# Four of the nine down products of the experts in three f32r passes, and the layer norm of their half on ScalarE

## The chip, the cores and the metric

One core of a Trainium2 chip runs the whole kernel. Its engines are TensorE (PE, with its weight loads as PEld), VectorE (DVE), ScalarE (ACT), GpSimd (POOL) and SyncE (SP, which here issues all the transfers). The metric is the device time of one execution in microseconds, and lower is better.

## What is computed

Two halves over 32 x 256 tokens of width 128, fp32 in and out, each a residual around a layer norm.

```python
x = x + attn(layernorm(x))          # 16 heads of 8, window of 128 keys
x = x + ffn(layernorm(x))           # below, per token

scores = sigmoid(x @ gate_w.T)                       # 16 experts
topk_idx, topk_weight = gate(scores)                 # best 2 of 4 groups, then best 4 experts
g = einsum('th,eih->eti', x, gate_proj)              # 64 inner units per expert
u = einsum('th,eih->eti', x, up_proj)
expert_out = einsum('eti,ehi->eth', silu(g) * u, down_proj)
y = sum over the 4 chosen of topk_weight * expert_out
shared = (silu(x @ shared_gate_w.T) * (x @ shared_up_w.T)) @ shared_down_w.T
return y + shared
```

All 16 experts are computed for every token. The weight of an expert that wasn't chosen is zero.

## The kernel before

The attention half runs first, in 16 steps of 512 tokens (`STEPS`, `TOK`), then the experts' half in 16 steps `d` of 512 tokens. What sets the order is the program text alone: each engine has its own queue, written out by hand, and counted semaphores between the queues.

A step of the experts' half has nine products `p`: eight pairs of experts (`NP` = 8, 2 x 64 inner units on 128 partitions) and the shared expert. For each of them:

- TensorE, `up(d, p)` (L1551): the gate and the up projection, each as three f32r passes. The operands were split beforehand into a high part, rounded to f32r, and a low part, the rest: `whigh`, `wlow` and `xh`, `xl`. The passes are high x high (L1560), high x low (L1561) and low x high (L1562), into `ps_max` and `ps_sc`, two banks each.
- ScalarE, `silus` (L769): silu of the gate projection.
- VectorE, `gate` (L1099): times the up projection, into one of two `gated` tiles.
- GpSimd, `weigh` (L612): times the routing weight, which has been spread over the partitions by a transfer (`spread`), into one of three tiles `inter`. It waits until the down product three before has freed the tile.
- TensorE, `down(d, p)` (L1565): one fp32 matmul with `wd`, added up in `ps_c` over the nine products. TensorE's queue holds it behind the up products of the third pair after: iteration `p` of the loop at L1644 issues `up(d, p)` and then the down product three before. In the iterations 0, 1 and 2 these are the last three down products of the step before.

Beside this, each step prepares others. Its layer norm for step d+3 has statistics on VectorE (L838, L845), then on GpSimd the inverse deviation (`inverse_deviation`, L497, in two 128x4 instructions), `centre` (L504) and `normalise` (L509) after the weighing of pairs 1, 2 and 3. TensorE transposes the result at p = 7 (`transpose_x1`), ScalarE copies its high part (`high_x`) and VectorE subtracts the low part (`low_x`). The routing for step d+2 has products on TensorE (`route`, at p = 1), two activations on ScalarE (`scores_of_experts`, after the silu of p = 3) and some thirty small instructions on VectorE between its gates: `sum_logits`, `clip` and `invert` after gate(2), `choices` (with `score` and `choice`) and `sum_pairs` after gate(3), the result of the step before (`add_y`) and `sum_groups` after gate(4), the group masks after gate(5), `find_best` and `mark_best` (with the copy `needles`) after gate(6), `choose_experts` (with `chosen`) and `shares` (with `total1`) after gate(7), then `gate_shared`. `up(d, p)` can't start before the gate two before it is done, since that frees its banks.

Between the halves, `last` interleaves the end of the attention with the transposes of the experts' weights (`transpose_weight`, L1475). ScalarE takes each bank (`take_weight`, L736) in the order router, shared, gate and up, down (two banks), and then the routing weights of step 0. These go to DRAM and come back spread over the partitions in a transfer of 1 MB (`store_weight`, `load_spread`), and the first `weigh` waits for it.


Of the kernel before, what the change touches and what calls it, by code (L numbers as in the profile page):

```python
# [6 lines left out]
FP32 = mybir.dt.float32  # L7
# [12 lines left out]
def build_block(nc, x, w_in, b_in, w_out, b_out, gate_w, e_bias, gate_proj, up_proj, down_proj,  # L20
# [46 lines left out]
    with ctx:  # L67
        def sb(name, shape, dt):
            return ctx.enter_context(nc.sbuf_tensor(name, shape, dt))
# [4 lines left out]
        def sem(name):  # L74
            return ctx.enter_context(nc.semaphore(name))
# [47 lines left out]


        NP = NE // 2
        TOPK, SCALING = 4, 2.5


# [12 lines left out]
        wlow = sb("wlow", [P, 2 * NP + 1, P], F32R)  # L141
        wrt = sb("wrt", [P, 2, NE], F32R)
        wd = sb("wd", [P, NP, E], FP32)
        wds = sb("wds", [I, E], FP32)
        xh = [sb(f"xh{p}", [P, TOK], F32R) for p in range(3)]
        xl = [sb(f"xl{p}", [P, TOK], F32R) for p in range(3)]
# [128 lines left out]
        gated_ready = sem("gated_ready")  # L275
        down_done = sem("down_done")
        inter_ready = sem("inter_ready")
        yT_ready = sem("yT_ready")
        y_tr_done = sem("y_tr_done")
        result_ready = sem("result_ready")  # L280
# [38 lines left out]
        def after(engine, semaphore, value):  # L319

            if value > 0:
                engine.wait_ge(semaphore, value)
# [153 lines left out]
        def _(pool):  # L476
            n_const = [0]

            def made():

                n_const[0] += 1
                return n_const[0]
# [10 lines left out]
            pool.wait_ge(const_ready, made())  # L493
            nc.gpsimd.memset(eps[:, :], EPS).then_inc(const_ready, 1)
            pool.wait_ge(const_ready, made())
            pool.sem_inc(ident_ready, 1)
            def inverse_deviation(i):  # L497

                pool.wait_ge(stats_ready, i + 1)
                nc.gpsimd.tensor_tensor(veps[:, :], meanvar[:, :, 1], eps[:, :], ALU.add).then_inc(pool_chain, 1)  # L500
                pool.wait_ge(pool_chain, 3 * i + 1)
                nc.gpsimd.tensor_tensor(rstd[:, :], veps[:, :], minus_half[:, :], ALU.pow).then_inc(pool_chain, 1)
# [96 lines left out]
            layer_norm(STEPS + 1)  # L599
            layer_norm(STEPS + 2)  # L600

            def scale_weight(d):

                if not valid(d):
                    return
                pool.wait_ge(share_ready, d + 1)
                after(pool, weight_tr_done, d)
                nc.gpsimd.tensor_tensor(weight[:, :, :], chosen[:, :, :],
                                        share[:, :].unsqueeze(2).to_broadcast([P, NT, NE]), ALU.mult
                                        ).then_inc(weight_ready, 1)  # L610
# [8 lines left out]
                                        ).then_inc(inter_ready, 1)  # L619

            scale_weight(0)
            scale_weight(1)
            for d in range(STEPS):
                more = d + 3 < STEPS
                for p in range(NP):
                    weigh(d, p)
                    if p == 1 and more:
                        inverse_deviation(STEPS + d + 3)
                    if p == 2 and more:
                        centre(STEPS + d + 3)  # L630
                    if p == 3 and more:
                        normalise(STEPS + d + 3)
                scale_weight(d + 2)


# [1 line left out]
        def _(act):  # L637
# [98 lines left out]
            def take_weight(n):  # L736
                dst, cols = WEIGHT_BANKS[n]
                act.wait_ge(fw_done, n + 1)
                rows = slice(0, {"sh_down": I, "weight": NE}.get(dst[0], P))
                nc.scalar.copy(high_of(dst), ps_max[n % 2][rows, 0:cols]).then_inc(fw_high, 1)  # L740


            def high_x(d):
# [25 lines left out]
            def silus(d, p):  # L769

                n = (NP + 1) * d + p
                act.wait_ge(g_done, n + 1)
                after(act, gated_ready, n - 1)
                rows = slice(0, P) if p < NP else slice(0, I)
                nc.scalar.activation(silu[n % 2][rows, :], ps_max[n % 2][rows, :], ACT.Silu).then_inc(silu_ready, 1)  # L775

            def take_y(d):

# [43 lines left out]
            for d in range(STEPS):  # L822
                if d > 0:
                    high_x(d + 2)
                for p in range(NP + 1):
                    silus(d, p)
                    if p == 2:
                        if d > 0:
                            take_y(d - 1)
                        take_weights(d + 1)  # L830
                    if p == 3:
                        scores_of_experts(d + 2)
# [390 lines left out]
        def _(pe):  # L1223
# [341 lines left out]
            def down(d, p):  # L1565

                if p == 0:
                    after(pe, yT_ready, d)
                if p < NP:
                    pe.wait_ge(inter_ready, NP * d + p + 1)  # L1570
                    last = mm(ps_c[:, :], wd[:, p, :], inter[p % 3], start=(p == 0), stop=False)  # L1571
                else:
                    pe.wait_ge(gated_ready, (NP + 1) * (d + 1))
                    last = mm(ps_c[:, :], wds[:, :], inter[p % 3][0:I, :], start=False, stop=True)  # L1574
                last.then_inc(down_done, 1)
# [64 lines left out]
            pe.wait_ge(probs_ready, 2 * UNITS * STEPS)  # L1640
            pe.wait_ge(fw_high, len(WEIGHT_BANKS))
            pe.wait_ge(fw_low, N_SPLIT)

            for d in range(STEPS):  # L1644
                for p in range(NP + 1):
# [40 lines left out]
```

## Time and profile before

| | us |
|---|---|
| median of 3 runs (756.61 to 762.22) | 761.21 |
| the profiled execution | 758.62 |
| its span, first to last instruction | 756.8 |
| experts' half, from its first down product to the end | 407.1 to 756.8 |
| mean granted clock of TensorE | 0.972 |

The rows come from the one profiled execution, so sums of rows are to be held against 758.62. "Busy" is the time in which an engine has an instruction running. A timeline row gives start, duration, engine, line, what is written from what is read, and the count of instructions merged in the row. Matmuls overlap in the records: a pass that holds the array for about 0.23 us is recorded as 0.39, so the pitch of the starts counts.

### The profile page before, as it was taken

To read this page: it belongs to the slowest core of one execution; us is meant where nothing else is said; L and a number is where in the kernel's file an instruction comes from. 1 tells how busy PE (TensorE), PEld (TensorE's weight loads), DVE (VectorE), ACT (ScalarE), POOL (GpSimd) and SP (SyncE) were. 2 spreads that over 40 slices of the span, in tenths; PEclk is the share of its full clock that TensorE was granted. 3 is DMA by queue.
4 is the path that set the end of the run, shared out by engine and by line. 5 is a ranking of instruction groups with operands and counts; after the bars stand their busy time and mean duration, and the time that the engine had idled before them with its cause. 6 is when DMAs were issued, how large, how long until landed. Compare 5 with 4: busy or idle time off the path is not lost.

```text
span 756.8 us, 21746 instructions
## 1 busy us (share of the span) xinstructions
PE 706.9 (93%) x8499; PEld 472.2 (62%) x8499; DVE 585.8 (77%) x1741; ACT 362.4 (48%) x739; POOL 306.4 (40%) x327
## 2 busy tenths in 40 slices
PE   4597999999999999999778999999999999999997
PEld 2365666666666666666555666666666666666664
DVE  6776788888888888888577878887777888777632
ACT  2165566767776676667562332333333233333321
POOL 6410221222211222122215656566666656664543
PEclk9589899999999999999999999999999999999999
DMA  2125123333323222333118366654445666544550
GB/s 59 58 87 148 62 85 102 102 102 102 101 61 101 86 70 93 102 102 101 59 35 207 73 138 154 155 134 113 118 122 137 152 155 120 131 103 108 119 139 29
DMA packets 64837, 79.96 MB, mean 106 GB/s; under 512 B 10960, under 2 KB 38880, under 8 KB 64736
## 3 DMA queue, kind: packets, MB, share of 16 engines
q1 hardware_dynamic: 64736, 78.58, 39.9%
q8 instruction: 68, 1.11, 0.6%
q14 instruction: 33, 0.27, 0.1%
HBM read 61.00 MB, written 17.56 MB: 104 GB/s over the span
## 4 chain that ended last, share of the span: by engine, by line
PE 80%; DVE 7%; DMA 5%; ACT 4%; issue 2%; SPq 1%; POOL 1%; DVEq 0%; ACTq 0%; PEldq 0%
PE ps_c L1571 14%; PE ps_att L1356 7%; PE ps_sc L1330 6%; PE ps_max L1288 5%; PE ps_max L1560 4%; PE ps_max L1562 4%; PE ps_max L1561 4%; PE ps_sc L1306 4%; PE ps_sc L1561 4%; PE ps_sc L1562 4%; PE ps_sc L1560 4%; PE ps_a L1254 3%; ACT probs L683 3%; PE ps_c L1574 2%; PE ps_b L1247 2%
## 5 line engine op out<-in xcount | busy, mean ns | idle before, releaser
L618 POOL TENSOR_TENSOR probs<-probs,stacks 128x512 f32<-128x512 f32 x128 | 165.0, 1290 | 125.7 <-DVE probs L1105 75.4
L775 ACT ACTIVATE probs<-ps_max 128x512 f32<-128x512 f32 x144 | 86.2, 598 | 220.1 <-PE ps_max L1562 216.5
L886 DVE TENSOR_REDUCE chunkmax<-ps_max 128x16 f32<-128x512 f32 (+1 forms) x256 | 155.3, 648 | 37.9 <-PE ps_max L1269 37.8
L683 ACT ACTIVATE probs<-ps_sc 128x512 f32<-128x512 f32 x256 | 138.9, 595 | 48.6 <-PE ps_sc L1306 47.6
L1105 DVE TENSOR_TENSOR probs<-probs,ps_sc 128x512 f32<-128x512 f32 x128 | 87.3, 682 | 69.6 <-PE ps_sc L1562 26.4
L1571 PE MATMUL ps_c<-probs,wd 128*128 128x512 f32 x256 | 130.3, 592 | 1.3 <-POOL probs L618 1.3
L1560 PE MATMUL ps_max<-xh,whigh 128*128 128x512 f32 x144 | 93.7, 650 | 2.9 <-DVE probs L1105 2.1
L531 POOL TENSOR_TENSOR xres<-xin,cvec 128x512 f32<-128x512 f32 x16 | 20.6, 1287 | 141.1 <-DVE x L938 140.7
L1330 PE MATMUL ps_sc<-stacks 32*64 32x192 f16 (+2 forms) x2048 | 64.4, 232 | 9.5 <-ACT probs L683 2.7
L1356 PE MATMUL ps_att<-probs,stacks 128*32 128x192 f32 (+1 forms) x1536 | 70.2, 317 | 0.0
L1288 PE MATMUL ps_max<-hl,qdiag 32*128 32x160 f16 (+4 forms) x1024 | 50.9, 220 | 16.0 <-DVE chunkmax L886 9.7
L1330 PEld LDWEIGHTS ps_sc<-stacks 32*64 32x64 f16 x2048 | 36.6, 105 | 42.2 <-ACT probs L683 27.0
L500 POOL TENSOR_TENSOR veps<-meanvar,eps 128x4 f32<-128x4 f32 x32 | 6.4, 201 | 136.7 <-DVE meanvar L850 136.7
L1561 PE MATMUL ps_max<-xl,whigh 128*128 128x512 f32 x144 | 56.9, 395 | 0.0
L1562 PE MATMUL ps_max<-xh,wlow 128*128 128x512 f32 x144 | 56.9, 395 | 0.0
L1571 PEld LDWEIGHTS ps_c<-probs,wd 128*128 128x128 f32 x256 | 48.2, 189 | 13.6 <-POOL probs L618 1.7
L1288 PEld LDWEIGHTS ps_max<-hl,qdiag 32*128 32x128 f16 x1024 | 32.7, 95 | 35.8 <-DVE chunkmax L886 18.9
L1356 PEld LDWEIGHTS ps_att<-probs,stacks 128*32 128x32 f32 x1536 | 43.9, 111 | 16.1 <-issue 2.9
L1561 PE MATMUL ps_sc<-xl,whigh 128*128 128x512 f32 x128 | 50.8, 397 | 0.0
L1562 PE MATMUL ps_sc<-xh,wlow 128*128 128x512 f32 x128 | 50.8, 397 | 0.0
L1560 PE MATMUL ps_sc<-xh,whigh 128*128 128x512 f32 x128 | 50.5, 394 | 0.0
L1306 PE MATMUL ps_sc<-edges,repeat 64*128 64x192 bf16 (+2 forms) x576 | 49.9, 243 | 0.0
(164 smaller groups left out, 1257.1 us busy)
## 6 DMA issues: line engine op xcount, KB each, us to landing
stacks<-weight_scratch SPq DMA_DIRECT2D x32, 1024.0 KB, 10.0
stacks<-qk_scratch SPq DMA_DIRECT2D x48, 256.0 KB, 3.4
qk_scratch<-hl SPq DMA_DIRECT2D x32, 256.0 KB, 3.4
xin<-in_L_attn_x_dram SPq DMA_DIRECT2D x16, 256.0 KB, 3.1
x_scratch<-x SPq DMA_DIRECT2D x16, 256.0 KB, 2.2
xin<-x_scratch SPq DMA_DIRECT2D x16, 256.0 KB, 8.9
xres<-x_scratch SPq DMA_DIRECT2D x16, 256.0 KB, 8.9
out_dram<-result SPq DMA_DIRECT2D x16, 256.0 KB, 8.8
```

Of the source, the lines that this page charges most:

```text
L618: nc.gpsimd.tensor_tensor(inter[p % 3], gated[p % 2], spread[d % 2][:, p, :], ALU.mult).then_inc(inter_ready, 1)
L683: nc.scalar.activation(dst[:, :], ps_sc[s][:, 0:dst.shape[1]], ACT.Exp, scale=SCALE).then_inc(probs_ready, 1)
L775: nc.scalar.activation(silu[n % 2][rows, :], ps_max[n % 2][rows, :], ACT.Silu).then_inc(silu_ready, 1)
L886: nc.vector.tensor_reduce(chunkmax[:, 2 * pair + m, at:at + CHUNKS[h]], ps_max[m][:, 0:BANK_COLS[h]].rearrange("p (n k) -> p n k", k=KB), ...
L1105: tt(gated[p % 2], silu[n % 2], ps_sc[n % 2][:, :], ALU.mult).then_inc(gated_ready, 1)
L1288: mm(ps_max[m][:, at:at + width], qdiag[rows, b * NB + n, :, :].rearrange("p c k -> p (c k)"), hl[rows, 0, 1, b * S + key0:b * S + key0 + ...
L1330: mm(dst, qkstack[p][rows, 1, jj, q0:q0 + TB], qkstack[p][rows, 0, jj, q0:q0 + QCOLS[m]].rearrange("p (n k) -> p n k", k=TB), start=(at == ...
L1356: last = mm(ps_att[32 * x:32 * x + 32, half * S + TB * m:half * S + TB * m + QCOLS[m]].rearrange("p (n k) -> p n k", k=TB), vdiag[p][:, (b ...
L1560: mm(bank[slot][:, :], whigh[:, q, :], xh[d % 3][:, :], start=True, stop=False)
L1561: mm(bank[slot][:, :], whigh[:, q, :], xl[d % 3][:, :], start=False, stop=False)
L1562: last = mm(bank[slot][:, :], wlow[:, q, :], xh[d % 3][:, :], start=False, stop=True)
L1571: last = mm(ps_c[:, :], wd[:, p, :], inter[p % 3], start=(p == 0), stop=False)
```

## The change

- `SPLIT_PAIRS` = (0, 2, 4, 6): the down products of these four pairs are made in three f32r passes, high x high, high x low and low x high. The other four pairs and the shared expert stay in fp32.
- For a split pair, ScalarE copies `inter` to `inter_high` after the silu of the next pair (`high_inter`), and GpSimd subtracts it from `inter` into `inter_low` after the weighing of the next pair (`low_inter`). TensorE's wait is for `inter_low_ready`. Both tiles are double.
- The down weights get high and low parts once: `take_weight` makes an extra copy per down bank and then waits for its copies, and `low_wd` subtracts twice on GpSimd, between the weights of step 0 and 1.
- In the experts' half, for the steps from 3 on, `centre` and `normalise` leave GpSimd. ScalarE does each in four activations of 128x128, one per group of 128 tokens, with minus the mean as bias and the inverse deviation as scale: `centre` after the silu of p = 4, `normalise` after that of p = 5 and the high part of pair 4. GpSimd keeps the inverse deviation, after pair 1, now behind `low_inter` of pair 0, and makes minus the mean with one more 128x4 instruction.

```diff
+        SPLIT_PAIRS = (0, 2, 4, 6)
@@ gpsimd
+            def deviation(d):
+                i = STEPS + d
+                inverse_deviation(i)
+                nc.gpsimd.tensor_tensor(minus_mean[:, :], meanvar[:, :, 0], minus_one[:, :], ALU.mult
+                                        ).then_inc(pool_chain, 1)
+                pool.wait_ge(pool_chain, 3 * i + 3)
+                pool.sem_inc(deviation_ready, 1)
+            def low_inter(d, p):
+                if p not in SPLIT_PAIRS:
+                    return
+                k = len(SPLIT_PAIRS) * d + p // 2
+                pool.wait_ge(inter_high_ready, k + 1)
+                nc.gpsimd.tensor_tensor(inter_low[p // 2 % 2][:, :], inter[p % 3],
+                                        inter_high[p // 2 % 2][:, :].bitcast(FP32), ALU.subtract
+                                        ).then_inc(inter_low_ready, 1)
+            def low_wd():
+                for n in range(2):
+                    pool.wait_ge(wd_high_ready, n + 1)
+                    part = slice(4 * n, 4 * n + 4)
+                    nc.gpsimd.tensor_tensor(wd_low[:, part, :], wd[:, part, :], wd_high[:, part, :].bitcast(FP32),
+                                            ALU.subtract).then_inc(wd_low_ready, 1)
             scale_weight(0)
+            low_wd()
             scale_weight(1)
             for d in range(STEPS):
-                more = d + 3 < STEPS
                 for p in range(NP):
                     weigh(d, p)
-                    if p == 1 and more:
-                        inverse_deviation(STEPS + d + 3)
-                    if p == 2 and more:
-                        centre(STEPS + d + 3)
-                    if p == 3 and more:
-                        normalise(STEPS + d + 3)
+                    if p > 0:
+                        low_inter(d, p - 1)
+                    if p == 1 and d + 3 < STEPS:
+                        deviation(d + 3)
                 scale_weight(d + 2)
@@ scalar
                 act.wait_ge(fw_done, n + 1)
                 rows = slice(0, {"sh_down": I, "weight": NE}.get(dst[0], P))
-                nc.scalar.copy(high_of(dst), ps_max[n % 2][rows, 0:cols]).then_inc(fw_high, 1)
+                if dst[0] == "down":
+                    nc.scalar.copy(wd_high[:, dst[1]:dst[1] + 4, :].rearrange("p n k -> p (n k)"), ps_max[n % 2][rows, 0:cols])
+                last = nc.scalar.copy(high_of(dst), ps_max[n % 2][rows, 0:cols])
+                last.then_inc(fw_high, 1)
+                if dst[0] == "down":
+                    act.wait_ge(fw_high, n + 1)
+                    act.sem_inc(wd_high_ready, 1)
+            def high_inter(d, p):
+                if p not in SPLIT_PAIRS:
+                    return
+                k = len(SPLIT_PAIRS) * d + p // 2
+                act.wait_ge(inter_ready, NP * d + p + 1)
+                after(act, down_done, (NP + 1) * ((k - 2) // len(SPLIT_PAIRS)) + 2 * ((k - 2) % len(SPLIT_PAIRS)) + 1)
+                nc.scalar.copy(inter_high[p // 2 % 2][:, :], inter[p % 3]).then_inc(inter_high_ready, 1)
+            def centre(d):
+                if not 3 <= d < STEPS:
+                    return
+                act.wait_ge(deviation_ready, d - 2)
+                for t in range(NT):
+                    last = nc.scalar.activation(xcent[:, t, :], xin[d % 2][:, t, :], ACT.Identity,
+                                                bias=minus_mean[:, t:t + 1])
+                last.then_inc(centred, 1)
+            def normalise(d):
...
+                for t in range(NT):
+                    last = nc.scalar.activation(xhat[:, t, :], xcent[:, t, :], ACT.Copy, scale=rstd[:, t:t + 1])
+                last.then_inc(xhat_ready, 1)
@@ scalar, the loop over the steps
                 for p in range(NP + 1):
                     silus(d, p)
+                    if p > 0:
+                        high_inter(d, p - 1)
+                    if p == 4:
+                        centre(d + 3)
+                    if p == 5:
+                        normalise(d + 3)
                     if p == 2:
@@ tensor, down(d, p)
                 if p < NP:
-                    pe.wait_ge(inter_ready, NP * d + p + 1)
-                    last = mm(ps_c[:, :], wd[:, p, :], inter[p % 3], start=(p == 0), stop=False)
+                    if p in SPLIT_PAIRS:
+                        k = len(SPLIT_PAIRS) * d + p // 2
+                        high, low = inter_high[p // 2 % 2][:, :], inter_low[p // 2 % 2][:, :]
+                        pe.wait_ge(inter_low_ready, k + 1)
+                        mm(ps_c[:, :], wd_high[:, p, :], high, start=(p == 0), stop=False)
+                        mm(ps_c[:, :], wd_high[:, p, :], low, start=False, stop=False)
+                        last = mm(ps_c[:, :], wd_low[:, p, :], high, start=False, stop=False)
+                    else:
+                        pe.wait_ge(inter_ready, NP * d + p + 1)
+                        last = mm(ps_c[:, :], wd[:, p, :], inter[p % 3], start=False, stop=False)
```

## Rows read from the trace of the kernel before

**Rows 1.** The page, busy us of each engine over the span
```profile
PE 706.9 (93%) x8499; PEld 472.2 (62%) x8499; DVE 585.8 (77%) x1741; ACT 362.4 (48%) x739; POOL 306.4 (40%) x327
```

**Rows 2.** Table by stage: stretch, length, busy by engine, granted clock, DMA, GB/s
```profile
410.00:431.00 21.00, 18.66 (x75) 11.90 (x74) 18.17 (x53) 5.71 (x10) 14.03 (x14) 1.00 0.51 114
...
519.00:541.00 22.00, 22.00 (x91) 14.76 (x90) 17.97 (x56) 7.23 (x15) 13.77 (x14) 1.00 0.56 134
```

**Rows 3.** Timeline of TensorE, one step of the experts' half: start, us, what
```profile
519.80 1.02 PE L1571 MATMUL ps_c<-probs,wd 128*128 128x512 f32 x2
...
522.05 1.02 PE L1571 MATMUL ps_c<-probs,wd 128*128 128x512 f32 x2
...
534.54 0.39 PE L1561 MATMUL ps_max<-xl,whigh 128*128 128x512 f32 x1
...
541.82 0.59 PE L1571 MATMUL ps_c<-probs,wd 128*128 128x512 f32 x1
```

**Rows 4.** The chain that ended last: start, us, what
```profile
519.96 0.86 PE ps_c L1571 x2
...
523.07 0.44 PE ps_b L1582 x4
```

**Rows 5.** Groups of instructions by form, GpSimd and ScalarE: busy, mean ns
```profile
L618 POOL TENSOR_TENSOR probs<-probs,stacks 128x512 f32<-128x512 f32 x128 | 165.0, 1290 | 125.7 <-DVE probs L1105 75.4 <-PE ps_c L1571 31.3 <-PE ps_c L1574 13.6
L505 POOL TENSOR_TENSOR xcent<-xin,meanvar 128x512 f32<-128x512 f32 x32 | 33.4, 1044 | 0.0
...
L750 ACT CAST xh<-ps_att 128x512 fp32r<-128x512 f32 x13 | 7.4, 568 | 0.0
...
L711 ACT COPY bvB<-bv 128x128 f32<-128x128 f32 x1 | 0.3, 305 | 0.0
```

**Rows 6.** Timeline of VectorE in that step
```profile
520.91 0.23 DVE L1013 SCALAR_TENSOR_TENSOR score<-tanh_over,sigma_below 128x64 f32<-128x64 f32 x1
521.17 1.20 DVE L1017 SCALAR_TENSOR_TENSOR choice<-score,bias 128x64 f32<-128x64 f32 x1
522.40 1.15 DVE L1026 TENSOR_TENSOR pair_sums<-choice 128x48 f32<-128x48 f32 x3
523.47 0.68 DVE L1105 TENSOR_TENSOR probs<-probs,ps_sc 128x512 f32<-128x512 f32 x1
...
527.46 0.68 DVE L1105 TENSOR_TENSOR probs<-probs,ps_sc 128x512 f32<-128x512 f32 x1
...
528.49 1.05 DVE L1075 COPY needles<-top 128x16 f32<-128x16 f32 x1
...
530.29 0.68 DVE L1105 TENSOR_TENSOR probs<-probs,ps_sc 128x512 f32<-128x512 f32 x1
```

**Rows 7.** Timeline of GpSimd in that step
```profile
520.97 1.32 POOL L618 TENSOR_TENSOR probs<-probs,stacks 128x512 f32<-128x512 f32 x1 [0.49 <-PE ps_c L1571]
522.24 1.04 POOL L515 TENSOR_TENSOR xhat<-xcent,rstd 128x512 f32<-128x512 f32 x1
...
528.22 1.29 POOL L618 TENSOR_TENSOR probs<-probs,stacks 128x512 f32<-128x512 f32 x1 [1.02 <-DVE probs L1105]
```

**Rows 8.** Timeline of ScalarE in that step
```profile
519.94 0.25 ACT L758 ACTIVATE tanh_over<-over 128x64 f32<-128x64 f32 x1
...
526.48 0.60 ACT L775 ACTIVATE probs<-ps_max 128x512 f32<-128x512 f32 x1 [1.65 <-PE ps_max L1562]
```

**Rows 9.** Timelines of ScalarE, GpSimd and TensorE between the halves
```profile
389.72 1.18 ACT L740 COPY wd<-ps_max 128x512 f32<-128x512 f32 x2 [0.58 <-PE ps_max L1503]
391.10 0.58 ACT L740 COPY weightT<-ps_max 16x512 f32<-16x512 f32 x1 [0.19 <-PEq L1494]
...
405.77 2.49 POOL L618 TENSOR_TENSOR probs<-probs,stacks 128x512 f32<-128x512 f32 x2 [5.20 <-DMA stacks<-weight_scratch]
...
407.09 1.12 PE L1571 MATMUL ps_c<-probs,wd 128*128 128x512 f32 x2 [1.30 <-POOL probs L618]
```

**Rows 10.** Timeline of TensorE at the experts' first passes, granted clock 0.50
```profile
398.53 0.63 PE L1560 MATMUL ps_sc<-xh,whigh 128*128 128x512 f32 x1
```

More of the change, by code:

```diff
@@ L143, in build_block @@
         wd = sb("wd", [P, NP, E], FP32)
+        wd_high = sb("wd_high", [P, NP, E], F32R)
+        wd_low = sb("wd_low", [P, NP, E], F32R)
+        inter_high = [sb(f"inter_high{n}", [P, TOK], F32R) for n in range(2)]
+        inter_low = [sb(f"inter_low{n}", [P, TOK], F32R) for n in range(2)]
+        minus_mean = sb("minus_mean", [P, NT], FP32)
+        minus_one = sb("minus_one", [P, NT], FP32)
         wds = sb("wds", [I, E], FP32)
@@ L277, in build_block @@
         inter_ready = sem("inter_ready")
+        inter_high_ready = sem("inter_high_ready")
+        inter_low_ready = sem("inter_low_ready")
+        wd_high_ready = sem("wd_high_ready")
+        wd_low_ready = sem("wd_low_ready")
+        deviation_ready = sem("deviation_ready")
+        centred = sem("centred")
         yT_ready = sem("yT_ready")
@@ L495, in _ @@
             pool.wait_ge(const_ready, made())
+            nc.gpsimd.memset(minus_one[:, :], -1.0).then_inc(const_ready, 1)
+            pool.wait_ge(const_ready, made())
             pool.sem_inc(ident_ready, 1)
@@ L775, in silus @@
                 nc.scalar.activation(silu[n % 2][rows, :], ps_max[n % 2][rows, :], ACT.Silu).then_inc(silu_ready, 1)
+            def high_inter(d, p):
[14 more added lines that the diff above has]
+            def normalise(d):
+                if not 3 <= d < STEPS:
+                    return
+                act.wait_ge(centred, d - 2)
+                act.wait_ge(xtr_done, STEPS + d - len(BANK_OF_X) if d > 3 else STEPS + 1)
+                if d == 3:
+                    act.wait_ge(fw_done, BANK_OF_X[2] + 1)
+                for t in range(NT):
+                    last = nc.scalar.activation(xhat[:, t, :], xcent[:, t, :], ACT.Copy, scale=rstd[:, t:t + 1])
+                last.then_inc(xhat_ready, 1)
             def take_y(d):
@@ L1642, in _ @@
             pe.wait_ge(fw_low, N_SPLIT)
+            pe.wait_ge(wd_low_ready, 2)
             for d in range(STEPS):
```

## The prediction

> **What bounds the kernel now.** I read the summary of the page first: TensorE is busy for 93% of the span, VectorE for 77% [rows 1]. Then the table by stage: in the experts' half (from about 407 us) a step of 512 tokens keeps TensorE busy for all of its time at a full granted clock, VectorE for 18.0 of 22.0 us, GpSimd for 13.8, ScalarE for 7.2 [rows 2]. The TensorE timeline gives the length of a step: the first down product of one step starts at 519.80 and that of the next at 541.82, so 22.02 us [rows 3]. TensorE is the bound today, but the two engines that feed it have little slack, and the list by engine says where.
>
> **The gain on TensorE.** In the chain that ended last an fp32 down product takes 0.86 us [rows 4]. Two products of neighbouring pairs stand 2.25 us apart (519.80 and 522.05 [rows 3]): six passes and one product, so a pass is (2.25 - 0.86) / 6 = 0.232. Three passes cost 0.70 and save 0.16. Four per step: 0.64, and if nothing else moved a step would take 21.38 us. Over 16 steps that is 10.3 us, the whole possible gain; the layer norm's move removes nothing from TensorE.
>
> **What is added elsewhere.** Durations: the low part on GpSimd is a subtract of two 128x512 operands in SBUF. No such subtract is in the trace. The multiply of that shape (`weigh`, L618) takes 1.29, the layer norm's subtract with a broadcast operand (L505) 1.04 [rows 5]. I take 1.29 and keep 1.04 as the lower end; back to back they follow at 1.25. ScalarE's 128x512 copy is 0.57 [rows 5]. Its 128x128 copy takes 0.31 [rows 5]; pieces of the same work overlap by about 0.06, so four layer norm activations take about 1.0 us, twice per step. GpSimd loses 2 x 1.04 and gains 4 x 1.29 plus a 128x4 product of 0.2: 13.8 + 3.3 = 17.1 of 21.4 us. ScalarE goes from 7.2 to 7.2 + 4 x 0.57 + 2 x 1.0 = 11.5. VectorE loses and gains no instruction. By busy time all of it fits; what decides is the order.
>
> **VectorE waits for GpSimd's operands.** Four kinds of VectorE instruction of a step that have only SBUF operands take about 1 us or more for 64 or fewer elements, and end when a GpSimd instruction ends: `choice` 521.17 to 522.37, GpSimd's product until 522.29; the three `pair_sums` 1.15 together, the first until after the 1.04 us product from 522.24; `needles` 528.49 to 529.54, GpSimd until 529.51; `chosen` (L1087) in the same way. `score`, just before a product started, took 0.23 [rows 6, 7]. So each costs the remainder of GpSimd's instruction, and back to back GpSimd instructions hold one after another: just one waiting VectorE instruction gets through at each boundary.
> The Trainium skill says the same in "SBUF — State Buffer", section "Who interferes with whom": VectorE instructions with two SBUF inputs, and copies and tensor_scalar in a 2-port mode, are fully blocked by a GpSimd instruction that reads SBUF. These rows agree; by that rule the added subtracts block more of them, `total1` below too.
>
> **The walk through a step,** in us after the first down product's start (0 = 519.80). TensorE without a stall, from six passes per up (1.39; the shared one 0.70), 0.70 or 0.86 per down product and 0.44 per four transposes [rows 4]: up(4) at 0.70, down(1) 2.09, transposes 2.95, up(5) 3.39, down(2) 4.78, up(6) 5.48, down(3) 6.87, up(7) 7.73, down(4) 9.12, transposes 9.82, up(8) 10.26, down(5) 10.95, up(0) of the next step 11.81, down(6) 13.20, up(1) 13.90; from there to the next zero 7.51 (one pass before 534.54, to 541.82 [rows 3]).
> - In the steady step GpSimd does weigh(1), low(0), the deviation (as now 1.3, plus 0.2), and weigh(2) from -0.9 to 0.4. ScalarE's `high_inter` of pair 2 waits for that and ends at 1.1, and `scores_of_experts` behind it at 1.4, where it now ends at 0.4 (519.94 plus 0.25 [rows 8]). GpSimd's weigh(3) starts at 1.0, so `score` no longer slips in before it: it ends at 2.35, and `choice` behind low(2) at 3.6 (low(2) runs 2.25 to 3.55).
> - `pair_sums` is free then (0.4 for three), so gate(4) starts at 3.98, against 3.67 now (523.47 [rows 6]). A gate takes 0.68 and the weighing starts 0.07 behind it (527.46 + 0.68, 528.22 [rows 6, 7]): weigh(4) ends at 6.0, ScalarE's high part at 6.65, its `normalise` at 7.6, and only then silu(6), which now runs at 6.7 (526.48 [rows 8]): until 8.2. VectorE would be ready for gate(6) at 3.98 + 3.99 = 7.97 (the distance from 523.47 to 527.46 [rows 6]); it starts at 8.25.
> - From gate(6) to gate(7) VectorE needs 2.83 (527.46 to 530.29 [rows 6]), in which weigh(6) blocks `needles`, as now. gate(7) starts at 11.08 (now 10.49).
> - Pair 6's low part is queued behind weigh(7) on GpSimd: 11.08 + 0.69 + 0.07 + 1.25 + 1.29 = 14.38. down(6), which today has waited for nothing, waits in TensorE's queue until 14.43: a stall of 1.23 where 0.64 was gained. All other products of the step are behind it. The other three split pairs have their low part in time: low(4) ends at 8.8 for 9.12, low(2) at 3.55 for 4.78, low(0) 2.3 before its product.
> - `chosen` gets through at weigh(7)'s end (13.19), `total1` (L1094, a tensor_scalar of SBUF operands) meets low(6). No row has it under a GpSimd instruction; free it costs nothing more (gate_shared ends before 13.90 + 1.23), blocked it puts gate_shared at 14.69 to 15.38 and up(1), which waits for it, at 15.45 instead of 15.13. The nearest row is `needles`, a small copy, which is blocked: I take 15.45.
> - The step: 15.45 + 7.51 = 22.96, or +0.94 against 22.02. Lower end: silu(6) not late and `total1` free, 21.38 + 0.95 = 22.33, +0.31. With subtracts of 1.04, low(2) and low(6) each give 0.25 back: 22.0 to 22.1, nothing gained or lost.
>
> **Start and end.** At the start the experts' first product waits for the 1 MB spread load (landing 405.77), which follows from the weights' copy at 391.10, two 0.59 copies behind which stood `wd` [rows 9]. Two more high copies stand before it: +1.0 (391.10 to 392.1), and all that follows moves. The `low_wd` subtracts (1.3 each) run at 391 to 394 while GpSimd is idle: nothing. Then weigh(0) runs from 406.8 to 408.05 (it starts at 405.77 now), high(0) 408.7, weigh(1) 409.3, low(0) 410.5: the first down product starts at 410.55, not 407.09 [rows 9], +3.45. ScalarE is in order, so silu(2) and the transposed weights' copy wait behind high(0); the latter's load has still 10 us to spare. The first step's other waits stay about as long as now: +3.5 in all. The steps d = 1 to 13 give 13 x 0.94 = 12.2. Step 14 has no routing on VectorE: -0.64. In the last one low(6) ends 3.6 after up(7) and only 2.26 of TensorE's work covers it: -0.64 + 1.35 = +0.7.
> Sum: 3.5 + 12.2 - 0.6 + 0.7 = 15.8; on the profiled execution's 758.6 (span 756.8) 774.4. That execution lies 2.6 below the median of the runs shown (761.2) and 1.0 below the mean of all four; I add 1: 775. Between the step's ends (+0.31 and +0.94) the same sum is 766 to 775, and 787 if ScalarE's activations with per-partition operands take twice as long (1.0 more per step, through silu(6)).
>
> **Rivals.**
> 1. *Order and operands bind, as walked*: 775, its own range 766 to 787. For it: the four blocked kinds, and that the gain needs gate(7) at 9.85 where it stands at 10.49 already. Chance 0.58.
> 2. *The subtract is as short as 1.04, or one blocked instruction slips through*: steps stay at about 22.0, the start costs 3.5: 763 (758 to 767). Against it: the row with two full operands is 1.29. Chance 0.24.
> 3. *TensorE's gain arrives* (other side: faster): VectorE reaches gate(7) by 9.85 after the first down product, 0.64 before today's 10.49, so that low(6) ends by 13.20. It would take `choice` and `pair_sums` both unblocked, 1.0 + 0.7. Then 759.6 - 10.3 + 3.5 = 753; without the start's 3.5, 749. For it: xhat and xcent leave GpSimd. Against it: low(2) stands where xhat stood. Chance 0.12.
> 4. *The clock falls in the new stall.* At half clock a pass is recorded as 0.63 [rows 10], against 0.39 [rows 3]. Seven slow passes per step, about as many as the first ones at 397 us, would add 7 x 0.24 = 1.7, so 775 + 22 = 797. Against it: in 410 to 431 us TensorE was idle 2.3 us at a granted clock of 1.00 [rows 2]. Chance 0.06.
>
> **Chances.** What this kernel's measurement can tell from no change is about 1%, 7.6 us. Rival 3 lies mostly around 753.6, so faster 0.08; same takes its rest, rival 2 and the low edge of 1: 0.30; slower 0.62. The range leaves out most of rivals 3 and 4: 756 to 787.
>
> **What would show each step.** Right: the down products' f32r passes 0.23 apart; TensorE idle once per step, about 1.2 us, before the first pass of pair 6's product, released by GpSimd's subtract; `score` and `choice` over 0.6 us each, `pair_sums` short; step length 22.6 to 23.0; the first down product near 410.5. Wrong: steps of 21.4 with gate(7) unchanged (rival 3), subtracts of 1.04 (rival 2), a granted clock under 0.95 in the steady steps (rival 4), or a stall before another pair, which would mean that I placed the late part wrongly.

## The result and the profile after

| | us |
|---|---|
| before, median of 4 | 761.7 |
| changed kernel, median of 4 (779.3 to 785.9) | 782.9 |
| its profiled execution, span | 779.3, 777.6 |
| ratio | 1.027, 95% interval 1.024 to 1.031 |

The changed kernel is slower by 2.7%. The prediction said 775 us and slower, range 756 to 787. Here and below the ratios leave out the few executions that took over 1.5% more than the fastest of their kernel.

The summary of the page of the changed kernel; first the busy time of each engine, as in [rows 1]:

```profile
PE 709.7 (91%) x8563; PEld 482.4 (62%) x8563; DVE 591.3 (76%) x1741; ACT 430.8 (55%) x909; POOL 363.0 (47%) x381
...
PE 68%; POOL 10%; DVE 8%; ACT 6%; issue 4%; DMA 3%; SPq 0%; POOLq 0%; ACTq 0%; DVEq 0%
```

The second line is the page's shares of the chain that ended last, by engine. GpSimd has grown by 57 us and ScalarE by 68, and GpSimd is now 10% of the chain, where it was 1%. The table by stage shows a step of the experts' half, to hold against [rows 2]:

```profile
505.60:528.80 23.20, 22.18 (x95) 15.29 (x94) 18.38 (x56) 11.97 (x26) 16.85 (x17) 1.00 0.54 126
```

GpSimd works 16.85 us of the step, costed at 17.1, and ScalarE 11.97, costed at 11.5. TensorE is idle for 1.0 us of a step that now lasts 23.2, at a full granted clock. (The records of its passes overlap, so by the starts of the passes the stalls come out longer.) Where, the TensorE timeline of the changed kernel shows (start, us, what), to hold against [rows 3]:

```profile
506.21 0.40 PE L1657 MATMUL ps_c<-inter_high,wd_high 128*128 128x512 f32 x1
506.45 0.39 PE L1658 MATMUL ps_c<-inter_low,wd_high 128*128 128x512 f32 x1
506.68 0.40 PE L1659 MATMUL ps_c<-inter_high,wd_low 128*128 128x512 f32 x1
506.92 0.39 PE L1643 MATMUL ps_max<-xh,whigh 128*128 128x512 f32 x1
...
520.77 0.50 PE L1657 MATMUL ps_c<-inter_high,wd_high 128*128 128x512 f32 x1 [0.91 <-POOL inter_low L632]
521.10 0.39 PE L1658 MATMUL ps_c<-inter_low,wd_high 128*128 128x512 f32 x1
521.33 0.40 PE L1659 MATMUL ps_c<-inter_high,wd_low 128*128 128x512 f32 x1
521.82 0.47 PE L1643 MATMUL ps_max<-xh,whigh 128*128 128x512 f32 x1
...
529.41 0.40 PE L1657 MATMUL ps_c<-inter_high,wd_high 128*128 128x512 f32 x1
```

The three f32r passes follow each other and the next up at 0.23 us: the saving on TensorE is there, 506.21 to 506.92 is 0.71. But pair 6's product starts at 520.77, 14.56 after the first one and not 13.20, and what it waited for is GpSimd's subtract. The step is 529.41 - 506.21 = 23.20.

GpSimd and VectorE in the same step, to hold against [rows 7] and [rows 6]. L660 is the weighing, L632 the low part, L1188 the gates, L1195 `gate_shared`, L1177 `total1`:

```profile
507.24 1.29 POOL L660 TENSOR_TENSOR probs<-probs,stacks 128x512 f32<-128x512 f32 x1 [0.53 <-DVE probs L1188]
508.49 1.28 POOL L632 TENSOR_TENSOR inter_low<-probs,inter_high 128x512 fp32r<-128x512 f32 x1
...
518.20 1.29 POOL L660 TENSOR_TENSOR probs<-probs,stacks 128x512 f32<-128x512 f32 x1 [1.54 <-PE ps_c L1662]
519.45 1.27 POOL L632 TENSOR_TENSOR inter_low<-probs,inter_high 128x512 fp32r<-128x512 f32 x1
```

```profile
507.96 0.66 DVE L1096 SCALAR_TENSOR_TENSOR score<-tanh_over,sigma_below 128x64 f32<-128x64 f32 x1
508.65 1.19 DVE L1100 SCALAR_TENSOR_TENSOR choice<-score,bias 128x64 f32<-128x64 f32 x1
509.88 0.41 DVE L1109 TENSOR_TENSOR pair_sums<-choice 128x48 f32<-128x48 f32 x3
510.20 0.68 DVE L1188 TENSOR_TENSOR probs<-probs,ps_sc 128x512 f32<-128x512 f32 x1
...
514.61 0.69 DVE L1188 TENSOR_TENSOR probs<-probs,ps_sc 128x512 f32<-128x512 f32 x1 [0.51 <-ACT probs L821]
...
517.44 0.68 DVE L1188 TENSOR_TENSOR probs<-probs,ps_sc 128x512 f32<-128x512 f32 x1
...
519.86 0.88 DVE L1177 TENSOR_SCALAR total<-total 128x4 f32<-128x4 f32 x1
520.77 0.18 DVE L1180 RECIPROCAL share<-total 128x4 f32<-128x4 f32 x1
520.98 0.69 DVE L1195 TENSOR_TENSOR probs<-probs,ps_max 64x512 f32<-64x512 f32 x1
```

The last two GpSimd rows show the cause: the weighing of pair 7 starts 0.08 after the end of gate(7), and the low part of pair 6, whose input had been complete since 517.3, comes behind it. (The tag in the row names a product of TensorE. The program has that weighing wait for gate(7) and for pair 4's product only, and pair 4's last pass starts at 515.80, so gate(7), which ends at 518.12, is what it waited for.) `total1`, 170 ns in the kernel before, takes 0.88 under that subtract.

ScalarE in the same step, to hold against [rows 8]:

```profile
512.30 0.62 ACT L830 CAST inter_high<-probs 128x512 fp32r<-128x512 f32 x1 [1.19 <-POOL probs L660]
512.82 1.27 ACT L851 ACTIVATE xhat<-xcent,rstd 128x128 f32<-128x128 f32 x4
514.00 0.58 ACT L821 ACTIVATE probs<-ps_max 128x512 f32<-128x512 f32 x1
```

And the change of halves, to hold against [rows 9], from the timelines of ScalarE, GpSimd and TensorE:

```profile
391.78 0.59 ACT L781 CAST wd_high<-ps_max 128x512 fp32r<-128x512 f32 x1
...
392.97 0.58 ACT L782 COPY weightT<-ps_max 16x512 f32<-16x512 f32 x1
...
407.60 2.48 POOL L660 TENSOR_TENSOR probs<-probs,stacks 128x512 f32<-128x512 f32 x2 [5.55 <-DMA stacks<-weight_scratch]
...
411.36 0.50 PE L1657 MATMUL ps_c<-inter_high,wd_high 128*128 128x512 f32 x1 [4.22 <-POOL inter_low L632]
...
412.40 0.63 PE L1643 MATMUL ps_max<-xh,whigh 128*128 128x512 f32 x1
412.83 0.63 PE L1644 MATMUL ps_max<-xl,whigh 128*128 128x512 f32 x1
```

The last two rows are 0.43 apart and not 0.23: after TensorE had stood idle for 4.2 us, its granted clock was 0.50 from 412 to 415 us, and 1.00 again from 416 on. The kernel before stood idle for 1.3 us there and kept 1.00.

Where the 20.8 us between the spans (756.8 and 777.6) are: the attention half of this execution ran 0.9 us longer (the transposes of the first down bank start at 389.93, not 389.06; before them the change adds one small memset and nothing else). The way from there to the first `take_y` is 44.89 us, not 40.89: 4.0. From the first to the thirteenth, 278.9 against 264.3: 14.55. The rest, 63.9 against 62.5: 1.4.

### The profile page after: what moved, and what is told of

It is laid out like the page before. It is cut to its first block, busy times and chain, and to the rows that moved or that the text cites. A ratio compares the mean times of both kernels' runs of the same rounds, so it can differ in the third digit from the quotient of the medians.

```text
span 777.6 us, 22175 instructions
## 1 busy us (share of the span) xinstructions
PE 709.7 (91%) x8563; PEld 482.4 (62%) x8563; DVE 591.3 (76%) x1741; ACT 430.8 (55%) x909; POOL 363.0 (47%) x381
## 4 chain that ended last, share of the span: by engine, by line
PE 68%; POOL 10%; DVE 8%; ACT 6%; issue 4%; DMA 3%; SPq 0%; POOLq 0%; ACTq 0%; DVEq 0%
PE ps_att L1439 8%; PE ps_sc L1413 6%; POOL probs L660 6%; PE ps_c L1662 5%; PE ps_max L1371 5%; PE ps_sc L1389 4%; PE ps_max L1643 3%; ACT probs L723 3%; PE ps_a L1337 3%; POOL inter_low L632 3%; PE ps_max L1644 3%; PE ps_max L1645 3%; PE ps_sc L1644 2%; PE ps_sc L1643 2%; PE ps_sc L1645 2%
## 5 line engine op out<-in xcount | busy, mean ns | idle before, releaser
L660 POOL TENSOR_TENSOR probs<-probs,stacks 128x512 f32<-128x512 f32 x128 | 164.5, 1286 | 97.6 <-DVE probs L1188 70.8
L1188 DVE TENSOR_TENSOR probs<-probs,ps_sc 128x512 f32<-128x512 f32 x128 | 87.5, 684 | 73.5 <-ACT probs L821 33.8
L632 POOL TENSOR_TENSOR inter_low<-probs,inter_high 128x512 fp32r<-128x512 f32 x64 | 81.7, 1277 | 0.0
L830 ACT CAST inter_high<-probs 128x512 fp32r<-128x512 f32 x64 | 39.7, 620 | 65.4 <-POOL probs L660 65.4
L1643 PE MATMUL ps_max<-xh,whigh 128*128 128x512 f32 x144 | 72.8, 505 | 2.9 <-DVE x L1021 0.5
L1662 PE MATMUL ps_c<-probs,wd 128*128 128x512 f32 x128 | 65.5, 593 | 0.0
```

Of the source, the lines that this page charges most:

```text
L632: nc.gpsimd.tensor_tensor(inter_low[p // 2 % 2][:, :], inter[p % 3], inter_high[p // 2 % 2][:, :].bitcast(FP32), ALU.subtract).then_inc(in ...
L660: nc.gpsimd.tensor_tensor(inter[p % 3], gated[p % 2], spread[d % 2][:, p, :], ALU.mult).then_inc(inter_ready, 1)
L1188: tt(gated[p % 2], silu[n % 2], ps_sc[n % 2][:, :], ALU.mult).then_inc(gated_ready, 1)
L1643: mm(bank[slot][:, :], whigh[:, q, :], xh[d % 3][:, :], start=True, stop=False)
L1662: last = mm(ps_c[:, :], wd[:, p, :], inter[p % 3], start=False, stop=False)
```

## The experiments

The theory: TensorE's gain is real and is lost to order. Pair 6's low part stands behind the last weighing on GpSimd, that weighing is late because GpSimd and ScalarE hold up VectorE, and up(1) then waits for `gate_shared`. The rival explanations: the layer norm on ScalarE costs it; GpSimd simply has too much work, in whatever order; the late start. Most steps of a kernel repeat to 0.05 us, while the whole time scatters by 1%. Much of the scatter lies in the attention half, which is the same in all these kernels: the transposes of the first down bank start at 386.96 us in the profiled execution of one of them (mean granted clock 0.975) and at 395.03 in that of another (0.963). So the step is the sharper measure: the median distance between the `take_y` copies on ScalarE, which is 22.03 us before and 23.2 in the changed kernel. Where three or five rounds were run, the ratio to the kernel before is given too. It is to the runs of the kernel before that were made beside them, whose median is 761.7 us for the first four and 762.4 for the last two.

| kernel | step, us | expected | time, us | ratio (95%) |
|---|---|---|---|---|
| before | 22.03 | | 761.7 | |
| changed | 23.20 | 22.96 | 782.9 | 1.027 (1.024 to 1.031) |
| layer norm alone | 22.11 | 22.0 | 759.8 | 0.998 (0.995 to 1.002) |
| split alone | 23.52 | 24.2 | 785.1 | 1.030 (1.022 to 1.037) |
| without pair 6 | 22.50 | 22.2 | 769.0 | 1.008 (1.004 to 1.012) |
| low(6) first | 22.41 | 22.3 | 768.7 | 1.010 (1.007 to 1.014) |
| normalise later | 22.80 | 22.8 | 776.8, one run | |
| total in PSUM | 22.88 | 22.9 | 775.9, one run | |
| unblocked | 21.43 | 21.4 | 753.9 | 0.989 (0.985 to 0.992) |
| unblocked, earlier start | 21.43 | 21.4 | 756.2 | 0.993 (0.989 to 0.996) |

### The two halves of the change, each alone

```diff
-        SPLIT_PAIRS = (0, 2, 4, 6)
+        SPLIT_PAIRS = ()
-            low_wd()
-                if dst[0] == "down":
-                    nc.scalar.copy(wd_high[:, dst[1]:dst[1] + 4, :].rearrange("p n k -> p (n k)"), ps_max[n % 2][rows, 0:cols])
```

> The kernel before with the layer norm's move to ScalarE alone: all nine down products in fp32, no high or low parts of inter or wd. Theory (order: pair 6's low part behind the last weighing, and VectorE's blocked instructions, set the loss): TensorE was and stays the bound, the experts' step stays at 22.0 us and the time at that of before, 761 us within 0.5%. VectorE's pair_sums should no longer be blocked and gate(4) come about 0.7 us earlier, without effect. Rival (ScalarE's eight layer norm activations are themselves the loss): a step of 22.4 or more, 767 us or more.

Measured: 0.998 of the kernel before, the interval holds 1. In the timeline of VectorE of this kernel `pair_sums` is short:

```profile
517.82 1.20 DVE L1094 SCALAR_TENSOR_TENSOR choice<-score,bias 128x64 f32<-128x64 f32 x1
519.05 0.41 DVE L1103 TENSOR_TENSOR pair_sums<-choice 128x48 f32<-128x48 f32 x3
519.37 0.68 DVE L1182 TENSOR_TENSOR probs<-probs,ps_sc 128x512 f32<-128x512 f32 x1
```

Gate(4) starts 2.92 us after the step's first down product (516.45), where it was 3.67, and nothing comes of it, since TensorE was the bound. The move to ScalarE costs nothing by itself and wins nothing that the whole time shows. That the step is 22.11 and not 22.03 has not been explained; against it stands the first step, which is 1.5 us shorter (22.68 us from the first weighing to the first `take_y`, 24.18 before).

```diff
                     if p > 0:
                         low_inter(d, p - 1)
-                    if p == 1 and d + 3 < STEPS:
-                        deviation(d + 3)
+                    if p == 1 and d + 3 < STEPS:
+                        inverse_deviation(STEPS + d + 3)
+                    if p == 2 and d + 3 < STEPS:
+                        centre(STEPS + d + 3)
+                    if p == 3 and d + 3 < STEPS:
+                        normalise(STEPS + d + 3)
```

> The changed kernel with the layer norm back on GpSimd as before (centre after pair 2's weighing, normalise after pair 3's), the split products kept. Theory: GpSimd's order is the bound, so two more instructions of 1.04 us in it delay weigh(3), low(2) and gate(4) (to about 5.4 us after the first down product, from 3.99) and then all behind: a step of about 24.2 us instead of 23.2, 796 us. TensorE should then stall before down(4) as well. Rival (the layer norm on ScalarE, which delays silu(6), is the loss): a step of 22.7 or less, under 776 us.

Measured: 23.52, slower than the changed kernel's 23.20 and not faster, so the rival is out; but 0.7 less than I had worked out. GpSimd's timeline in this kernel has the reason:

```profile
508.14 1.30 POOL L660 TENSOR_TENSOR probs<-probs,stacks 128x512 f32<-128x512 f32 x1
509.39 1.05 POOL L520 TENSOR_TENSOR xcent<-xin,meanvar 128x512 f32<-128x512 f32 x1
510.40 1.29 POOL L660 TENSOR_TENSOR probs<-probs,stacks 128x512 f32<-128x512 f32 x1
511.65 1.27 POOL L632 TENSOR_TENSOR inter_low<-probs,inter_high 128x512 fp32r<-128x512 f32 x1
512.88 1.04 POOL L530 TENSOR_TENSOR xhat<-xcent,rstd 128x512 f32<-128x512 f32 x1
```

The first down product is at 509.38, so weigh(3) at 510.40 is 1.02 behind it, as in the changed kernel (1.03): `centre` fits in the gap before it, which my walk had overlooked. Only `normalise` costs, through VectorE: `pair_sums` takes 1.15 again and gate(4) starts at 4.73 (514.11), 0.74 later than in the changed kernel. But silu(6) isn't late any more, so most of it comes back: gate(6) starts at 8.55 (517.93) against 8.40. The expected stall before down(4) is there, but small: its low part ends at 518.90 and the product starts at 9.58 (518.96), against 9.13. So once products are split, the layer norm's place on ScalarE is worth 0.32 us a step; alone it is worth nothing.

### The late low part: without it, and in another order

```diff
-        SPLIT_PAIRS = (0, 2, 4, 6)
+        SPLIT_PAIRS = (0, 2, 4)
-                nc.scalar.copy(inter_high[p // 2 % 2][:, :], inter[p % 3]).then_inc(inter_high_ready, 1)
+                nc.scalar.copy(inter_high[k % 2][:, :], inter[p % 3]).then_inc(inter_high_ready, 1)
```

> The changed kernel with three split pairs (0, 2, 4); pair 6's product stays in fp32 (its buffers alternate by count). Theory: the stall of 1.2 us before down(6) goes, 0.16 of the gain goes with it, and total1 is no longer blocked; chosen still is, so gate_shared ends near 14.65 and up(1) waits some 0.45: a step of about 22.2 us, 769 us. Rival (GpSimd's total load sets the step): a quarter of the loss goes, 22.9 us, 778 us.

Measured: a step of 22.50, 769.0 us. With pair 6 unsplit the step becomes 0.70 shorter though TensorE has 0.16 more to do. The rival's 22.9 is out, but 22.2 was too low by 0.3. TensorE's own work is now 21.6 (21.4 and the 0.16), and two waits make up the other 0.9. The longer is that of up(1) for `gate_shared`, 0.54 by the starts, in TensorE's timeline of this kernel:

```profile
515.69 0.47 PE L1643 MATMUL ps_max<-xh,whigh 128*128 128x512 f32 x1 [0.37 <-DVE probs L1195]
```

The other is a wait that no expectation had: up(0) can't start before gate(7) is done, which is at 512.72, and starts 0.18 late, at 512.81. After each of the two waits the first pass takes 0.31 to 0.32 until the next and not 0.23, another 0.08.

```diff
                 for p in range(NP):
+                    if p == 7:
+                        low_inter(d, p - 1)
                     weigh(d, p)
-                    if p > 0:
+                    if 0 < p < 7:
                         low_inter(d, p - 1)
```

> The changed kernel with one change of order on GpSimd: pair 6's low part before pair 7's weighing instead of behind it. The same instructions on every engine. Theory: low(6) ends near 12.4 after the first down product and down(6) at 13.2 waits for nothing; the weighing behind it now blocks total1 (until 13.7), so gate_shared ends near 14.7 and up(1) waits 0.85: a step of about 22.3 us, 770 us. Rival (GpSimd's load, not its order): the step stays at 23.2 us, 783 us.

Measured: 22.41, 768.7 us. Not one instruction is added, taken away or made shorter, and two thirds of the loss are gone (0.79 of 1.17 us a step). That settles it between order and load for this part of the loss (the rival expected 23.2). The timelines of GpSimd, VectorE and TensorE in this kernel show both sides of the exchange:

```profile
514.23 1.27 POOL L632 TENSOR_TENSOR inter_low<-probs,inter_high 128x512 fp32r<-128x512 f32 x1 [0.73 <-ACT inter_high L832]
515.46 1.31 POOL L660 TENSOR_TENSOR probs<-probs,stacks 128x512 f32<-128x512 f32 x1
...
515.88 0.92 DVE L1179 TENSOR_SCALAR total<-total 128x4 f32<-128x4 f32 x1
...
516.53 0.39 PE L1659 MATMUL ps_c<-inter_high,wd_high 128*128 128x512 f32 x1
...
517.87 0.47 PE L1645 MATMUL ps_max<-xh,whigh 128*128 128x512 f32 x1 [0.48 <-DVE probs L1197]
```

Pair 6's product (516.53) waits for nothing. The weighing that is now behind holds `total1` in place of the subtract, and up(1) waits for `gate_shared`, 0.64 by the starts. With up(0) 0.18 late behind gate(7), as without pair 6, and 0.08 after each wait, that is all of the 0.98 us that are left over TensorE's 21.43.

### The other two links

```diff
-                    if p == 5:
+                    if p == 6:
                         normalise(d + 3)
```

> The changed kernel with one change of order on ScalarE: normalise after the silu of p = 6 instead of before it. Theory: gate(6) then starts when VectorE is ready for it, 8.0 us after the first down product instead of 8.4, gate(7) at 10.83 instead of 11.23, and the whole rest of the step follows: a step of 22.8 us instead of 23.2. Rival (ScalarE's place does not matter, GpSimd's port alone does): 23.2.

Measured: 22.80, 0.40 less, as worked out. Gate(6) starts at 7.80 after the first down product and gate(7) at 10.81, where they were at 8.40 and 11.23.

```diff
-        total = sb("total", [P, NT], FP32)
+        total = ps_a[:, ROUTE + 4 * NT * NE + NT * 4:ROUTE + 4 * NT * NE + NT * 5]
-                after(pe, route_dve, DVE_OPS * (d - 1) + 21)
+                after(pe, route_dve, DVE_OPS * d)
```

> The changed kernel with the 128x4 tile total in PSUM instead of SBUF, so that total1 (the tensor_scalar after chosen) reads no SBUF operand; TensorE's next route waits for it in turn. Theory: total1 is no longer held by GpSimd's low(6) (0.17 us instead of 0.88), gate_shared starts 0.7 us earlier, and up(1) waits only for down(6): a step shorter by 0.3 us, 22.9 us. Rival (the 0.88 us has another cause, or nothing waits for gate_shared): total1 stays at 0.88, or the step at 23.2.

Measured: 22.88, 0.32 less. VectorE's timeline of this kernel, at the same place of the step, while GpSimd's subtract runs as before:

```profile
518.28 1.27 DVE L1171 TENSOR_TENSOR chosen<-picked,score 128x64 f32<-128x64 f32 x1
519.59 0.23 DVE L1176 TENSOR_REDUCE ps_a<-chosen 128x4 f32<-128x64 f32 x1
519.85 0.16 DVE L1178 TENSOR_SCALAR total<-ps_a 128x4 f32<-128x4 f32 x1
```

0.16 us in place of 0.88 for the same four elements per partition, with the input in PSUM (the memory that TensorE sums into) and not in SBUF (the other on-chip memory): it was the SBUF operand that waited. The Trainium skill, "SBUF — State Buffer", section "Who interferes with whom", says that a tensor_scalar can enter a 2-port mode, and that such an instruction and one of GpSimd block each other for the whole instruction. No row of the kernel before had shown it for tensor_scalar; this trace agrees.

### All of it at once

The edits of the last three, and `picked` in PSUM beside `total`, so that `chosen` has one SBUF operand.

```diff
-        picked = sb("picked", [P, NT, NE], FP32)
+        picked = ps_a[:, ROUTE + 4 * NT * NE + NT * 5:ROUTE + 5 * NT * NE + NT * 5].rearrange("p (t n) -> p t n", t=NT)
```

> The changed kernel with all of these at once: pair 6's low part before pair 7's weighing, normalise after the silu of p = 6, and total and picked in PSUM so that neither chosen nor total1 has all its operands in SBUF. The arithmetic and the instruction counts are those of the changed kernel. Theory: gate(7) at 10.83, low(6) until 12.0, gate_shared until 13.5, each before TensorE needs it (11.81, 13.20, 13.90): no stall is left, and the step is TensorE's own 21.4 us. With the start 4 us later: about 756 us, 0.6% under the kernel before. Rival (GpSimd at 17 of 21 us of work can't keep up in any order): a step of 22.0 or more.

Measured: 21.43 us a step, 753.9 us, 0.989 of the kernel before (0.985 to 0.992). The table by stage of this kernel:

```profile
502.40:523.80 21.40, 21.40 (x95) 15.52 (x93) 16.69 (x57) 11.95 (x27) 16.79 (x17) 1.00 0.57 137
```

GpSimd does the same 16.8 us of work as in the changed kernel and TensorE has no idle time left. The single edits won 0.79, 0.40 and 0.32 us a step, the four together 1.77; `picked` in PSUM has no run of its own. The end of the step on VectorE:

```profile
514.73 0.68 DVE L1192 TENSOR_TENSOR probs<-probs,ps_sc 128x512 f32<-128x512 f32 x1
515.32 0.22 DVE L1171 TENSOR_TENSOR ps_a<-replaced,ps_a 128x64 f32<-128x64 f32 x1
515.58 0.22 DVE L1174 TENSOR_TENSOR chosen<-ps_a,score 128x64 f32<-128x64 f32 x1
```

Gate(7) is 10.83 after the first down product (503.90), and `chosen` takes 0.22 where it took 1.29. So the load of GpSimd is not the cause of any of the loss in the steps. The gain of the prediction's rival 3 arrives, and with gate(7) at 10.83, not by 9.85 as the prediction held it to need: that condition came from low(6) standing behind weigh(7).

Then two things more (and TensorE's wait for `wd_low_ready` moves to its first down product):

```diff
+                    if p == 3:
+                        scores_of_experts(d + 2)
                     if p > 0:
                         high_inter(d, p - 1)
@@ the end of last(now) on ScalarE
+                for m in range(2):
+                    act.wait_ge(fw_high, N_SPLIT + m + 1)
+                    nc.scalar.copy(wd_high[:, 4 * m:4 * m + 4, :].rearrange("p n k -> p (n k)"),
+                                   wd[:, 4 * m:4 * m + 4, :].rearrange("p n k -> p (n k)")).then_inc(wd_high_ready, 1)
```

> The kernel of the run e7_unblocked with two things more: scores_of_experts before the high part of pair 2 on ScalarE, and the high parts of the down weights copied from SBUF after ScalarE's last work of the attention, off the path of the routing weights (TensorE waits for them only before its first down product). Theory: the steps stay at 21.4 us, score is not held any more (0.23 us), and the spread load and the first down product come 1.0 us earlier than in that run: about 755 us, 0.8% under the kernel before. Rival (the late start is not due to the two copies): no earlier than in e7_unblocked.

Measured: 21.43 a step, 756.2 us, and 0.993 (0.989 to 0.996), which overlaps the run before; a gain of 1 us can't be told from it. The traces can be compared from the down banks' transposes on, without the attention half: from there to the end it is 367.7 us in the kernel before, 387.7 in the changed one, 362.0 in "unblocked" and 360.2 in this one. They show that the expectation of the start held: from the transposes to the first weighing it is 16.49 us (387.21 to 403.70), against 17.78 in the kernel of the run before and 16.71 in the one before the change. And TensorE, idle for 3.3 us before its first down product and not 4.1, keeps a granted clock of 1.00 behind it, where it fell to 0.50 in "unblocked"; from that product to the first `take_y` it is 20.63 us and not 21.32. The expectation on `score` was wrong:

```profile
516.77 1.29 DVE L1099 SCALAR_TENSOR_TENSOR score<-tanh_over,sigma_below 128x64 f32<-128x64 f32 x1
```

In the kernel before it started 0.06 us before weigh(3) [rows 6, 7]. Now weigh(3) is 0.14 earlier, since the f32r product that it waits for is shorter, and `score` (516.77) comes just behind it (516.68). ScalarE's part of its input was there at 516.04; VectorE itself gets to it only then. It ends 2.41 after the first down product, as in the changed kernel, so the high part that stood before `scores_of_experts` on ScalarE had cost it nothing.

## Why the prediction was right, and where it was short

The direction, the mechanism and its place were right, by the steps in the order of the prediction (times after the first down product):

| step of the prediction | predicted | changed kernel |
|---|---|---|
| GpSimd subtract 128x512 | 1.29 | 1.28 |
| three f32r passes | 0.70 | 0.71 |
| `score`, `choice` end | 2.35, 3.6 | 2.41, 3.63 |
| gate(4) starts | 3.98 | 3.99 |
| `normalise`, four activations | 1.0 | 1.27 |
| gate(6) starts | 8.25 | 8.40 |
| gate(7) starts | 11.08 | 11.23 |
| down(6) starts | 14.43 | 14.56 |
| `total1` blocked | yes | 0.88 us |
| up(1) starts | 15.45 | 15.61 |
| from there to the next step | 7.51 | 7.59 |
| step | 22.96 | 23.20 |

Rival 1 was the case. The choices at the open prices all fell as chosen: the two-operand duration and not the layer norm's 1.04, and `total1` blocked as `needles` is. In the steps no clock was lost (rival 4): the granted clock is 1.00 there. It did fall in a stall that the prediction had worked out and not looked at for this, the one before the first down product.

One reason in the walk was not needed: the prediction had `score` held because ScalarE's high part delays it and weigh(3) starts earlier. The last run shows that the second alone does it.

The size came out 25% short: 15.8 us of loss by the sum, 20.8 between the spans. Of the missing 5.0, 3.1 lie in the steps, 0.5 at the start, 0.9 in the attention half, 0.4 in one late step and the last 0.2 in the end. In the steps the term that was mis-sized is ScalarE's activation with a per-partition operand. I had priced it by the plain 128x128 copy at 0.31 [rows 5]; `centre` and `normalise` take 0.39 each, 1.27 for four, as the rows above show. With the high part's 0.62 for 0.57 that is why silu(6) started at 7.79 and gate(6) was 0.15 late. A pass after a stall takes some 0.08 more until the next than one in a row (521.82 to 522.12 is 0.30, against 0.23), which the 7.51, taken between passes in a row, didn't have. Together 0.24 a step, 3.1 us in 13 steps.

The start was 4.0 us instead of 3.5. Its two terms were right (the weights' copy 3.04 behind the bank's transposes in place of 2.04, and 3.76 from the landing to the first down product in place of 1.32). Together they are 3.4. What I had not worked out is the first step behind them: "the other waits stay about as long as now" was an assumption without a row. From the first down product to the first `take_y` it is 23.46 us, not 22.86, 0.6 more. Two things are in it that the kernel before didn't have, the granted clock of 0.50 from 412 to 415 us and a wait of 0.9 us for a low part (at 427.90); a wait of 2.1 us for VectorE (at 414.87 in the kernel before) is gone in return. The slow clock stands behind the first down product in all seven kernels in which TensorE was idle for 3.9 to 4.4 us before it, and in none of the three in which it was idle for 0.9, 1.3 and 3.3. No run changes the clock alone, so its share of the 0.6 stays open.

0.9 us of the difference between the profiled executions lies in the attention half and is none of the change's. What stays open: in each kernel with split products one step, the ninth between `take_y` copies, is 0.2 to 0.4 us longer than its neighbours, and adds 0.4 us in the changed kernel. (In "split alone" the second is longer too, by 0.2.) The traces show where it begins: gate(3) of that step starts 2.35 us after `take_y` and not 1.99, though ScalarE's and TensorE's part of its input came at the same time as in the other steps. It is as late in the two kernels without split products, where the step doesn't get longer, so there the slack took it up. Why it is late no run shows.

## What to carry over

Before giving an idle engine more work, walk its queue and not its busy share: the low part needed 1.3 us on an engine that was idle for a third of the step, and held the engine it served up for 1.4 us a step (14.56 against 13.20), because it was issued one instruction too late. When VectorE and GpSimd both work from SBUF, count what each new GpSimd instruction holds up; one tile of 16 bytes per partition moved to PSUM took 0.3 us off each step. A gain on the bounding engine is worth realising only together with the order that delivers it in time: the same split gave +2.7% and, in another order and with two tiles moved, -1.1%.

## What the runs showed of the hardware that I had not expected

- ScalarE's 128x128 activation with a per-partition bias or scale, from SBUF to SBUF, takes 0.39 us, a copy of that shape 0.31. A 128x512 cast from SBUF takes 0.62, from PSUM 0.57.
- GpSimd's subtract takes 1.28 us when it writes f32r, no more than its fp32 multiply of that shape (1.29).
- The blocking of VectorE does not scale with the blocked tile: 4 elements per partition waited 0.7 us.
- After 4.2 us without work TensorE's granted clock was 0.50 for about 3 us, and a pass took 0.43 us in place of 0.23; in the kernel in which it stood idle for 3.3 us at the same place the clock stayed at 1.00.
